# Capsule passes 2 and 3: the scaling of the shares moves from GpSimd to VectorE, and its sums and inverses from SBUF to PSUM

## What is computed

```python
xc = _l2norm(x.reshape(num_node, NUM_CAPS, dpc))    # 8 capsules of 16 features
z = xc[src]
u = xc
for _ in range(NITER):                              # 3 passes
    p = jnp.einsum('ecd,ecd->ec', z, u[trg])
    p = jax.nn.softmax(p / TAU, axis=1)
    msg = z * p[:, :, None]
    u = jax.ops.segment_sum(msg, trg, num_segments=num_node)
    u = _l2norm(u + xc)
```

## Time and profile before

| quantity | value |
| --- | --- |
| three runs | 6071.28, 6073.38, 6076.0 us (median 6073.38) |
| profiled execution, its time | 6063.14 us |
| profiled execution, its span | 6061.1 us |
| CAPS2 and CAPS3 in it | about 3039 to 4010 us of the span |
| engine shares of the span | PE 63%, VectorE 62%, ScalarE 27%, GpSimd 74% |

### The profile page before, as it was taken

How to read it: one execution, slowest core, us unless ns; L and a number is a source line. 1 busy time by engine, 2 the same in 40 slices (tenths; PEclk the granted TensorE clock), 3 DMA queues, 4 the chain that set the end, 5 groups by cost and what they waited for, 6 DMA issues and landing times. The chain is left out here.

```text
span 6061.1 us, 136817 instructions
## 1 busy us (share of the span) xinstructions
PE 3843.8 (63%) x27584; PEld 3353.5 (55%) x27585; DVE 3781.4 (62%) x9458; ACT 1650.8 (27%) x4107; POOL 4500.8 (74%) x5150
## 2 busy tenths in 40 slices
PE   1545555455555476777689989945665664676665
PEld 1445445455455465655578878845555553555544
DVE  5333333566566677777887787775555555666666
ACT  2000000112212333333455565531111113222222
POOL 6777777777777677777778888857777775777775
PEclk9766666667666688888899999977777776888887
DMA  4222222222222355555577777832222222222222
GB/s 125 69 73 71 71 71 69 66 70 73 70 73 69 114 175 169 178 173 171 173 243 250 249 225 248 253 105 69 73 70 73 71 71 54 71 73 73 74 70 98
DMA packets 462303, 702.23 MB, mean 116 GB/s; under 512 B 95985, under 2 KB 218110, under 8 KB 461778
## 3 DMA queue, kind: packets, MB, share of 16 engines
q0 software_dynamic: 125680, 259.25, 16.5%
q10 hardware_dynamic: 210816, 255.92, 13.1%
q1 hardware_dynamic: 125538, 184.63, 9.6%
HBM read 506.20 MB, written 189.54 MB: 115 GB/s over the span
## 5 line engine op out<-in xcount | busy, mean ns | idle before, releaser
L893 POOL DMA_INDIRECT u_parts<-table,src x3080 | 2906.2, 944 | 1043.6 <-issue 917.5
L969 PE MATMUL ps_sum<-u_parts,onehot 128*128 x2928 | 650.2, 393 | 632.2 <-SPq L741 555.2
L1525 DVE SCALAR_TENSOR_TENSOR onehot<-dst,minus_row,beside 128x512 f32<-128x512 f32 x1100 | 817.0, 744 | 305.5 <-issue 242.8
L969 PEld LDWEIGHTS ps_sum<-u_parts,onehot 128*128 128x128 f32 x2928 | 576.3, 293 | 702.7 <-issue 701.0
L893 POOL DMA_INDIRECT ring<-table,src x774 | 737.5, 953 | 265.3 <-issue 233.0
L969 PEld LDWEIGHTS ps_sum<-msg,onehot 128*128 128x128 f32 x4896 | 689.2, 212 | 306.3 <-issue 134.6
L969 PE MATMUL ps_sum<-msg,onehot 128*128 128x128 f32 x4896 | 749.3, 301 | 129.3 <-DVE msg L532 98.6
L969 PE MATMUL ps_u<-u_parts,onehot 128*128 x2928 | 522.7, 339 | 456.4 <-SPq L741 429.2
L969 PEld LDWEIGHTS ps_u<-u_parts,onehot 128*128 128x128 f32 x2928 | 469.9, 245 | 493.5 <-issue 492.9
L1832 DVE TENSOR_TENSOR zu<-ps_u,ring 128x512 f32<-128x512 f32 x732 | 503.1, 687 | 338.0 <-SPq L741 150.3
L1047 PE MATMUL ps_u<-WE_attr,attr_t 128*128 128x512 f32 x488 | 314.2, 731 | 333.0 <-ACT attr_t L1379 332.8
(11 more groups left out here) (224 smaller groups left out, 6510.2 us busy)
## 6 DMA issues: line engine op xcount, KB each, us to landing
ring<-z_rows SPq DMA_DIRECT2D x392, 256.0 KB, 3.7
ring<-table SPq DMA_DIRECT2D x6144, 0.5 KB
hot_rows<-hots ACTq DMA_DIRECT2D x244, 256.0 KB
hots<-hot_rows ACTq DMA_DIRECT2D x244, 256.0 KB, 3.5
z_rows<-ring SPq DMA_DIRECT2D x196, 256.0 KB
u_parts<-table,src POOLq DMA_INDIRECT x3080
table<-hots ACTq DMA_DIRECT2D x122, 256.0 KB
wide<-hot_rows ACTq DMA_DIRECT2D x122, 256.0 KB, 3.5
```

What stands on the lines that cost most here:

```text
L893: nc.gpsimd.indirect_dma_start(out=slot(p, c % slots)[:, t * P:(t + 1) * P], out_offset=None, in_=tables[p], in_offset=bass.IndirectOffset ...
L969: last = nc.tensor.matmul(sums[k % len(sums)][:, 0:P], lhsT=(onehot[:, k % HOTS, :, :] if hots_of is None else hots_of)[:, t, :], rhs=rows ...
L1525: V.scalar_tensor_tensor(out=buffers[k % len(buffers)], in0=per_row(dst[:, ds(chunk * TILES, TILES)], [P, TILES, P]), scalar=minus_row0[:, ...
```

## The change

VectorE gets a third operation for a pair of steps, behind the inverse: the scaling that GpSimd did. The sums and inverses that it reads move from the SBUF tile `psums` to 16 free columns of the PSUM bank `beside`. GpSimd keeps the messages and the adds. The new operation waits for its own inverse, and for the message of step s - 6, which is the last to read the slots of `prob_n` that it writes. No wait is added on TensorE, ScalarE or SyncE, and no DMA is touched.

```diff
@@ -232,6 +232,8 @@
         share_p = [beside[:, 3 * P + i * TILES * CAPS:3 * P + (i + 1) * TILES * CAPS] for i in range(2)]
+        sums_p = beside[:, 3 * P + 2 * TILES * CAPS:3 * P + 2 * TILES * CAPS + HOTS * TILES]\
+            .rearrange("p (i t) -> p i t", t=TILES)
@@ -855,15 +857,6 @@
                 def make(s, k, chunk):
-                    if k % 2 == 0:
-                        at = k % HOTS
-                        pool.wait_ge(exp_inverted, s + (G + 2))
-                        pool.wait_ge(msg_ready, s + (G - 2))
-                        nc.gpsimd.tensor_tensor(
-                            prob_n[:, at:at + 2, :].rearrange("p i (t c) -> p (i t) c", c=CAPS),
-                            prob[:, at:at + 2, :].rearrange("p i (t c) -> p (i t) c", c=CAPS),
-                            psums[:, at:at + 2, :].rearrange("p i t -> p (i t)").unsqueeze(2)
-                            .to_broadcast([P, 2 * TILES, CAPS]), ALU.mult).then_inc(share_ready, 2)
@@ -1807,7 +1800,7 @@
-                        V.tensor_reduce(psums[:, at:at + 2, :],
+                        V.tensor_reduce(sums_p[:, at:at + 2, :],
                                         prob[:, at:at + 2, :].rearrange("p i (t c) -> p i t c", c=CAPS),
                                         AX, ALU.add).then_inc(exp_summed, 2)
@@ -1815,7 +1808,17 @@
-                        V.reciprocal(psums[:, at:at + 2, :], psums[:, at:at + 2, :]).then_inc(exp_inverted, 2)
+                        V.reciprocal(sums_p[:, at:at + 2, :], sums_p[:, at:at + 2, :]).then_inc(exp_inverted, 2)
+
+                    def share_pair():
+
+                        at = (k - 3) % HOTS
+                        dve.wait_ge(exp_inverted, s + (G - 1))
+                        dve.wait_ge(msg_ready, s + (G - 5))
+                        V.tensor_tensor(prob_n[:, at:at + 2, :].rearrange("p i (t c) -> p (i t) c", c=CAPS),
+                                        prob[:, at:at + 2, :].rearrange("p i (t c) -> p (i t) c", c=CAPS),
+                                        sums_p[:, at:at + 2, :].rearrange("p i t -> p (i t)").unsqueeze(2)
+                                        .to_broadcast([P, 2 * TILES, CAPS]), ALU.mult).then_inc(share_ready, 2)
@@ -1847,6 +1850,7 @@
                     if whole_pair:
                         invert_pair()
+                        share_pair()
```

## The result

The changed kernel takes 6110.48 us (median of 6 runs, 6107.81 to 6113.12) against 6074.05 us (6 runs, 6071.28 to 6076.0): 1.006 of before, interval 1.0049 to 1.007. It is slower by 36 us, above the upper end of my range.

A forecast was written before the change was run, and what follows sets the result against it. VectorE was taken to pace the edge stretches; in the steady ones TensorE was near its floor, waiting 40 us for messages. -26 + 8 + 12 = -6 us gave 6067 us, eight in ten between 6046 and 6088.

The forecast's parts named there:

- What is added: VectorE's 244 new scalings: the next `zu` starts 0.36 us behind the inverse instead of 0.11, 0.28 a pair with PSUM.
- own wait: VectorE's scaling waiting for its own inverse's result: taken as 0.04 us, with GpSimd's 0.22 as upper bound.
- Steady stretches: hidden.: Full-clock middle of CAPS2 and CAPS3: VectorE's pair grows from 2.94 to 3.22 us, under TensorE's 3.30, hidden except behind heads.
- Rival 2: VectorE becomes the bound because the scaling holds its queue, 0.34 to 0.41 us a pair: +25 us, 6098; chance 0.20.
- A sign of being wrong: Steady steps that do not get shorter because another latency replaces the message; forecast was about 1.82 us a step.
- Heads: Starts of VectorE's loop rounds, where it is late already: 28 rounds at 0.28 us add 8 us.
- Edge stretches: Three stretches with norms and splits, VectorE setting the pace: 63 pairs at 0.28 us, 18, of which 12 us count.
- some takes it up: VectorE's 31 us free in the edge stretches absorb part of the 18 us added, leaving 12.
- The gain, 26 us: Steady stretches: messages come 0.25 us sooner, counted 0.22, so TensorE's 90 waits lose 20 us, queue relief 6 more.
- The new wait for an old message: VectorE's scaling waits for the message of step s - 6, long ended by then: costed at nothing.
- GpSimd as true bound: Relieved of 0.51 us a pair, GpSimd lets nearly all 40 us of message waits go: -24 us, 6049; chance 0.30.
- The rule of the Trainium skill: On VectorE the next operation starts only when the pipe is empty, so the scaling would hold the queue its whole duration.

The follow-up runs named there:

- slot_wait: Kernel before, GpSimd's scaling kept, plus an unread VectorE operation of 64 elements that waits for its pair's inverse: 1.0045 of before, CAPS2 and CAPS3 1003.8 us.
- slot: Kernel before, GpSimd's scaling kept, plus the same unread VectorE operation behind each pair's inverse, without a wait: 1.0011 of before, CAPS2 and CAPS3 969.8 us.
- extra_after: The change with two long-satisfied waits and three register operations behind the scaling, in the loop only: 1.0074 of before, CAPS2 and CAPS3 1027.5 us.
- inverse_early: The change with the inverse ahead of `logit` instead of behind it: 1.0012 of before, CAPS2 and CAPS3 972.5 us.
- before_early: Kernel before, GpSimd scaling, with the inverse ahead of `logit` in the loop only: 0.9976 of before, CAPS2 and CAPS3 946.4 us.
- sums_sbuf: The change with sums and inverses in SBUF instead of PSUM: 1.0052 of before, CAPS2 and CAPS3 997.9 us.
- hybrid: VectorE scales, inverse ahead of `logit`, for pairs 52 to 208 of each pass; GpSimd scales at the edges: 1.0004 of before, CAPS2 and CAPS3 962.5 us.

## Why the prediction was wrong, point by point

- **The step that failed** is the sum under "What is added": "So the next `zu` comes at 0.36 instead of 0.11: 0.25 us a pair, and 0.28 with a little for PSUM. Bounds: 0.13 (the bare slot) and 0.41 (own wait at 0.2)." Measured is 0.72 instead of 0.11, 0.61 a pair where a `zu` follows. The terms that I had were right: scaling 0.22, slot 0.08 to 0.13, and the own wait, for which slot_wait has 0.03 us behind the inverse's end against my 0.04. Two terms were missing. The larger is the queue work of the next `zu` (231 ns, with its gaps all of the 0.43 behind the scaling, where I had 0.13): hidden until then behind `logit`, it comes to lie behind the wait. The smaller is the second wait of the new operation, below. slot and slot_wait show the wait as cause, the queue's rows and extra_after show what is behind it. I took the 0.11 of the earlier trace rows for a price of the inverse, and it was one of an operation whose preparation had been done ahead.
- **How the miss divides.** I had -26 + 8 = -18 us for the steady stretches and 12 for the edges; measured are 10.8 in the loops and 26.8 at the edges (by slightly different cuts). Some 29 us of the miss lie in the loops and 15 at the edges.
- **"Steady stretches: hidden."** With 2.94 + 0.61 a pair would be 3.55 us; 3.52 was measured in one, over TensorE's 3.30. Rival 2, "VectorE becomes the bound", gave 0.36 a pair as the point from which it decides. It decided, by another way than named there: not the operation holding the queue, but the wait ahead of it. Its 6098 was short since even its 0.41 was. A sign of being wrong that I had named came: the loops' steps did not get shorter, 1.93 us (331.2 / 172) after 1.89.
- **Heads,** 28 x 0.28 = 8 us. Measured are 0.75 each, 20.9 us: branch and table load start behind the wait too. With them TensorE's wait for a message behind each head grew, from 9.0 to 16.6 us in the first loop.
- **Edge stretches,** 12 us, bounds 5 and 18 (26 with 0.41 a pair): 26.8 measured. That VectorE sets the pace there was right, and the price a pair was near, 0.32 where a piece of the norms follows and 0.43 where a `zu` does, against 0.28. What failed is "some takes it up": the 31 us of idle time took up nothing, and the 72 pairs' 25.6 us appear in full. inverse_early, with most of the wait hidden in the loops, still loses 16 us there.
- **The gain, 26 us.** Its mechanism held: the message came 0.20 us sooner where I said 0.25, and away from the heads TensorE's waits for messages in the first loop fell from 10.2 to 1.5 us. The heads took it back, so that in 3110:3458 it still waited 19.9 us (20.1 before). before_early shows that a gain is to be had, 16 us, when VectorE isn't slowed.
- **The new wait for an old message** was costed at nothing. It held nothing back, but it is a second wait on one instruction: with both waits the scaling starts 0.09 us behind the inverse's end (the change and sums_sbuf), with only one 0.03 (slot_wait). That is 0.06 a pair, 14 us of VectorE's time in 244 pairs, some of it taken up by idle time. No run takes this wait out of the change.
- **GpSimd as true bound** (rival 1) is refuted: with GpSimd relieved by 24 us in each loop, the change's loops are 11 us over those of before and the hybrid's 3 under; before_early, with all of GpSimd's work, has the shortest, 16 under.
- **PSUM,** "a little" in both places: about 0.01 us a pair.
- **The rule of the Trainium skill** that the prediction names is half of what stands there: the same paragraph of "The DRAIN you can't avoid" goes on that a next operation that is not held starts earlier. slot agrees with that half: `zu` starts 0.08 us behind an operation that lasts 0.17.

Still open: how much of the edges' 0.32 us a pair an operation with a single wait would keep in the change itself, and whether the hybrid's loss is the later message alone.

## What to carry to other kernels

On VectorE here, an operation added directly behind the one whose result it needs cost far more than its slot of 0.08 us: 0.32 where nothing was to be prepared behind it, and 0.61 where the register and address work of the *next* operation, which the profile of before shows as costing nothing, moved onto the path. So look in the trace at when the engine's queue instructions run: if during the operation ahead, price them as exposed before adding such a wait; and put an independent operation between producer and consumer. Where a message must come sooner, first try to move the producer earlier in its engine's order, which here cost no instruction and was worth more than moving work between engines.

## What the hardware showed that I had not expected

A 64-element operation takes 0.08 us of VectorE's queue without a wait and, with a wait for its predecessor, 0.11 us more ahead of it (0.22 instead of 0.11) and 0.35 us more behind it (0.43 instead of 0.08) where the next operation has registers to prepare; 0.05 more (0.14 instead of 0.09, medians at the edges) where it has not. The Trainium skill, VectorE: DVE Perf Modes, "The DRAIN you can't avoid", reports that semaphores after each of eight copies added nothing to them; the 34.0 us between slot and slot_wait disagree for small operations that wait for the one ahead, and the measurement decides. A register operation of 40 to 45 ns takes 0.07 to 0.09 us of the queue, and a second wait on an operation 0.06 us, though its semaphore was long satisfied. Placing 8 elements a partition in PSUM instead of SBUF made the sum and the inverse 9 and 11 ns longer, and a scaling that reads them no longer (222 against 226 ns).
